# The convolution's first loads move into the attention's last step, and the convolution opens the ternary feedforward

## The chip, the cores and the metric

The kernel runs on one core of a Trainium2 chip. A core has five engines with an instruction stream each: TensorE (PE, matrix products, which write to PSUM), VectorE (DVE), ScalarE (ACT), GpSimd (POOL) and SyncE (SP), which here issues nearly all the DMA transfers. The engines meet only through semaphores. The metric is the device time of one launch in microseconds (us), the median of the runs; lower is better.

## The reference, cut to what matters

The program is a decoder of six stages on x of shape (8, 256, 512), each with a residual and a layer norm. The last three are these; L is 512, because the convolution reads the (8, 256, 512) tensors as (batch, channels, length).

```
def attention1(x):            # 64 heads of 8, softmax over 256 keys, output projection
def convolution(k, v, q):     # k = v = context, q = x; B, HD, L = 8, 256, 512; head_dim 8, H = 32
    kv = einsum('bhil,bhjl->bijhl', k, v)
    y = irfft(rfft(kv, 2 * L) * rfft(ssm_kernel, 2 * L))[..., :L]
    out = einsum('bijhl,bhil->bjhl', y + kv * D, q)
def ternary_feedforward(x):
    h = gelu(silu(bitlinear158(x, w1, b1)))            # 512 -> 2048
    h = layer_norm(h, ln_g, ln_b)
    return bitlinear158(h, w2, b2)                     # 2048 -> 512
def bitlinear158(x, w, b):    # rms_norm of x, rounded to 8 bits by its row's peak; w rounded to -1, 0, 1
    return einsum('bsd,od->bso', act_quant(rms_norm(x)), weight_quant(w)) + b

x = layer_norm(x + attention1(x))
x = layer_norm(x + convolution(context, context, x))
x = layer_norm(x + ternary_feedforward(x))
```

## The kernel before, in words

`program` calls one function for each stage. A stage opens its tensors, runs one block in which each engine has a program written out by hand, and ends in a barrier of all engines; only then does the next stage's first instruction start. The order on each engine is the order of the code.

`attention1` works on eight sequences (B = 8, step b). In its last step SP sends the last two quantised pieces of the ternary weights (`send_piece`, out of `d_wq`), then stores the last four tiles of x (`store_x`) and waits until they have landed (`stored`).

`long_convolution` goes over NT = 16 pairs n of heads, h = 2n and 2n + 1 (SH = 32 heads). For each head, ACT copies contexts (`widen`, into `e_cx`) and puts them into PSUM (`put`, `e_pc`); DVE multiplies them (`products`, into `e_kv`); PE convolves them with a matrix of taps (`convolve`, from `e_toep`, into `e_py`: four PSUM banks, reused one for one, so that unit t of a head waits until DVE has read unit t of the head before); DVE multiplies the result by the queries (`weigh`, `e_qx`, into `e_planes`); ACT completes three small edges (`wraps`); POOL sums the planes (`sums`, in three additions of 1024, 512 and 256 elements a partition). For each pair, PE transposes the rows of x (`turn_x`, into `e_px`) which ACT copies into queries (`queries`), and transposes the sums back (`turn_z`, into `e_pz`) which DVE adds to x (`add`). The layer norm is left to ACT and POOL (`square`, `root`, `normal`). SP loads contexts (`e_ctr`, for two pairs at a time), taps and rows of x (`x_rows`) in the stage itself. The first convolution of PE stands ahead of its first `turn_x`.

`ternary_feedforward` takes 16 tiles of 128 rows in groups of GT = 4, as a software pipeline written as steps s, from -3 on. The opening of a group is: ACT squares the rows of its four tiles (`g_junk_x`), DVE takes their peaks (`group_peaks`), POOL makes a reciprocal root, DVE works out scales (`group_scales`, nine small operations in a row), and PE transposes them into `lrows`. The opening of a tile is: DVE scales and rounds it (`g_xq`), PE transposes it, ACT copies it (`g_q1f`), PE forms the first product (`g_p`: four matmuls with the bias in `g_bpart`, sixteen with `g_w`, into four PSUM banks), ACT applies silu and then gelu (`g_ha`). After that DVE and ACT do the layer norm (`g_hc`, `g_junk`), DVE rounds again, PE transposes and forms the second product (`g_pout`). Ahead of the first product stand the loads of all the weights and rows, the constants, and the split of the bias into a high and a low part (`g_bhigh`, `g_bpart`).

## Time and profile before

| | |
|---|---|
| median of 3 runs | 2001.24 us (1999.72 to 2002.05) |
| the profiled execution | 1995.72 us, span 1993.9 us |
| mean granted TensorE clock | 0.931 of full |
| busy share of the span | PE 87%, DVE 70%, ACT 52%, POOL 29% |
| `attention1` ends, convolution's first instruction | 1540.0, 1542.83 us |
| convolution's last instruction, feedforward's first | 1736.03, 1736.87 us |
| end of the span | 1993.9 us |

Busy shares are means over six stages with different limits, so they name no limit for any one of them. Instants are us from the span's start, and an instant at which one engine waits for another is what counts.

### The profile page before, as it was taken

The numbers are of one execution on the slowest core, as the hardware profiler recorded it, in microseconds if no ns is written. First come the engines' busy times: TensorE is split into PE (matmuls) and PEld (weight loads), VectorE is DVE, ScalarE is ACT, GpSimd is POOL, SyncE is SP. The second block draws the span as 40 slices with busy tenths as digits, with TensorE's granted clock in tenths as the row PEclk, the third lists the DMA queues.
The fourth block names the chain that finished last, engine by engine and source line by source line (L and its number), as shares of the span: only waits on it lengthen the run. The fifth ranks groups of instructions, "written<-read, shape, count | busy, mean of one in ns | idle before, by whom it ended". The sixth has DMA issues, their size and how long they took to land. (4 is left out here: it accounts for less than half of the span.)

```text
span 1993.9 us, 32229 instructions
## 1 busy us (share of the span) xinstructions
PE 1731.0 (87%) x11774; PEld 1339.0 (67%) x11774; DVE 1391.4 (70%) x2867; ACT 1033.5 (52%) x1936; POOL 569.2 (29%) x563
## 2 busy tenths in 40 slices
PE   4489999787869999999999997999996899677886
PEld 2255665423548999999999996788884677434443
DVE  8478888587955566666665655555664788649997
ACT  3426666624415444444444443564663344479995
POOL 6133332144110011001000002242342599723322
PEclk9669999956989999999999998999998899879998
DMA  6498888151612222222222234132232544120001
GB/s 168 41 98 98 94 96 91 35 173 39 216 38 64 57 67 67 78 67 67 77 64 70 77 102 148 68 124 79 75 118 76 134 101 90 54 91 11 22 22 32
DMA packets 148480, 163.87 MB, mean 82 GB/s; under 512 B 46240, under 2 KB 100384, under 8 KB 146528
## 3 DMA queue, kind: packets, MB, share of 16 engines
q1 hardware_dynamic: 143076, 151.85, 33.6%
q10 hardware_dynamic: 5248, 9.96, 1.4%
q8 instruction: 95, 1.56, 0.4%
q14 instruction: 61, 0.50, 0.1%
HBM read 116.86 MB, written 19.48 MB: 68 GB/s over the span
## 5 line engine op out<-in xcount | busy, mean ns | idle before, releaser
L1661 ACT ACTIVATE f_gate<-f_gu 128x256 f32<-128x256 f32 x264 | 98.5, 382 | 268.9 <-PE f_gu L1525 190.4
L1802 DVE TENSOR_TENSOR f_hid<-f_gate,f_gu 128x256 f32<-128x256 f32 x264 | 108.3, 420 | 156.0 <-ACT f_gate L1661 152.1
L570 DVE TENSOR_REDUCE a_rowmax<-a_ring 128x2 f32<-128x512 f32 x256 | 165.1, 687 | 52.5 <-PE a_ring L652 50.2
L2688 PE MATMUL e_py<-e_kv,e_toep 128*128 128x288 f32 x640 | 162.7, 410 | 15.6 <-DVE e_kv L2715 15.3
L523 ACT ACTIVATE a_prob<-a_sT 128x1024 f32<-128x1024 f32 x128 | 130.6, 1027 | 49.2 <-PE a_sT L641 49.2
L2688 PEld LDWEIGHTS e_py<-e_kv,e_toep 128*128 128x128 f32 x640 | 120.6, 192 | 47.7 <-issue 16.2
L1538 PE MATMUL f_gu<-f_lowh,f_bg 128*128 128x256 f32 x704 | 141.3, 283 | 5.2 <-POOL f_lowl L1443 5.0
L1525 PE MATMUL f_gu<-f_xhi,f_wg 128*128 128x256 f32 x704 | 131.4, 284 | 0.0
L1525 PE MATMUL f_gu<-f_xhi,f_wu 128*128 128x256 f32 x704 | 130.6, 283 | 0.0
L1807 DVE TENSOR_TENSOR f_hl<-f_hid,f_hh 128x768 fp32r<-128x768 f32 (+2 forms) x90 | 84.5, 939 | 55.9 <-ACT f_hh L1709 54.8
L1538 PEld LDWEIGHTS f_gu<-f_lowh,f_bg 128*128 128x128 f32 x704 | 115.7, 191 | 9.6 <-POOL f_lowl L1443 5.2
L1562 PE MATMUL f_pout<-f_wd,f_hh 128*128 128x512 f32 x352 | 111.2, 397 | 0.0
L1525 PEld LDWEIGHTS f_gu<-f_xhi,f_wg 128*128 128x128 f32 x704 | 109.8, 191 | 0.0
L1525 PEld LDWEIGHTS f_gu<-f_xhi,f_wu 128*128 128x128 f32 x704 | 109.6, 191 | 0.0
L2070 POOL TENSOR_TENSOR d_prob<-d_prob,d_rinv 128x1024 f32<-128x1024 f32 x32 | 60.4, 1894 | 169.7 <-DVE d_rinv L2364 169.7
L1709 ACT ACTIVATE f_hh<-f_hid 128x768 fp32r<-128x768 f32 (+2 forms) x90 | 74.9, 833 | 62.0 <-DVE f_hid L1802 62.0
L2127 PE MATMUL d_ring<-d_xh,d_w 128*128 128x256 f32 x512 | 97.8, 292 | 9.3 <-DVE d_offset L2401 8.3
L484 POOL TENSOR_TENSOR a_y<-a_y,cb 128x512 f32<-128x512 f32 x48 | 50.0, 1042 | 176.6 <-DVE a_y L552 176.6
L1525 PE MATMUL f_gu<-f_xlo,f_wg 128*128 128x256 f32 x352 | 99.9, 284 | 0.0
L1525 PE MATMUL f_gu<-f_xlo,f_wu 128*128 128x256 f32 x352 | 99.7, 283 | 0.0
L1538 PE MATMUL f_gu<-f_lowl,f_bg 128*128 128x256 f32 x352 | 99.6, 283 | 0.0
L652 PE MATMUL a_ring<-a_ks,a_qs 48*128 48x256 f32 x512 | 63.2, 324 | 40.1 <-DVE a_rowmax L570 20.5
(424 smaller groups left out, 4830.7 us busy)
## 6 DMA issues: line engine op xcount, KB each, us to landing
f_entry<-in_WdT SPq DMA_DIRECT2D x89, 256.0 KB, 2.8
d_staging<-in_w SPq DMA_DIRECT2D x16, 1024.0 KB, 5.7
a_qs<-a_hi SPq DMA_DIRECT2D x64, 128.0 KB, 7.4
a_ks<-a_hi SPq DMA_DIRECT2D x64, 128.0 KB, 6.0
e_toep<-lags SPq DMA_DIRECT2D x16, 512.0 KB, 3.8
f_entry<-in_Bg SPq DMA_DIRECT2D x89, 64.0 KB, 1.8
f_entry<-in_Bu SPq DMA_DIRECT2D x89, 64.0 KB, 2.0
cf<-in_xT SPq DMA_DIRECT2D x4, 1024.0 KB, 7.8
```

Source lines behind the costliest of these rows:

```text
L523: act.activation(prob[:, n % 4, :, :, :], sT[n % 2][:, :, :, :], ACT.Exp).then_inc(exp_done, 1)
L570: dve.tensor_reduce(rowmax[:, s % 2, :, e * SLOTS + j], ring[n % RING][:, :].rearrange("p (q t) -> p q t", t=T), AX.X, ALU.max, negate=Tru ...
L652: last = pe.matmul(dst[e][:, q * T:(q + 1) * T], qs[par][rows, pair, q * P:(q + 1) * P], ks[par][rows, pair, :], start=True, stop=True)
L1525: last = pe.matmul(gu[n % 3][:, w, :], ws[hw][:, k, f * P:(f + 1) * P], xs[b % 2][:, k, :], start=(m == 0 and w == 0), stop=(m == 3 * KT - ...
L1538: last = pe.matmul(gu[n % 3][:, w, :], bg[:, n % BR, h, w, :], xs[:, u, j - 1, w, :], start=False, stop=True, skip_group_check=True)
L1562: last = pe.matmul(pout[q][:, :], xs[:, t % 2, 0, cols], wd[:, n % WR, h, :], start=(f == 0 and m == 0), stop=(f == FT - 1 and m == 2))
L1661: act.activation(gate[:, i % 2, :], gu[n % 3][:, 0, :], ACT.Silu).then_inc(s_["gate_ready"], 1)
L1709: act.activation(hh[:, t % 2, lo:hi, :], hid[:, lo:hi, :], ACT.Copy).then_inc(s_["hh_ready"], 1)
L1802: dve.tensor_tensor(hid[:, j, :], gate[:, i % 2, :], gu[n % 3][:, 1, :], ALU.mult).then_inc(s_["hid_ready"], 1)
L1807: dve.tensor_tensor(hl[:, t % 2, lo:hi, :], hid[:, lo:hi, :], hh[:, t % 2, lo:hi, :], ALU.subtract).then_inc(s_["hl_ready"], 1)
L2127: last = pe.matmul(dst[:, f * T:(f + 1) * T], w[hw][:, wi, k, o * P:(o + 1) * P], xs[:, k, :], start=(m == 0), stop=(m == 3 * KT - 1))
L2688: last = pe.matmul(py[n % RING][:, 0:YS], toep[:, u, h % 2, (t - j) * P:(t - j + 1) * P], kv[:, h % 2, j, :, :].rearrange("p b c -> p (b c ...
```

## The change

Three things are changed. First, in the last step of `attention1` SP issues the convolution's first eight context loads and three loads of taps, once the last `v1` has been read; after the last store of x has landed it issues the first four loads of rows. In the convolution PE does `turn_x(0)` ahead of its first convolution. Second, SP issues the feedforward's loads within the convolution, one a pair from pair 4 on. Third, the convolution does the feedforward's opening: the constants and the split of the bias, squares for tiles 0 to 11, peaks and scales for tiles 0 to 3, the rounding and the transposes of tile 0, and, after its last convolution, the first product of tile 0. The feedforward then starts at step 0 with silu of tile 0. The four banks of `e_py` become those of the product, so the profile of the changed kernel calls them g_p.

The core of the diff:

```diff
+                    if b == B - 1:
+                        sp.wait_ge(s_["ring_read"], ring_at["v1", b] + 1)
+                        sp.wait_ge(s_["orow_added"], B * TB)
+                        sp.wait_ge(stored, 16 * (B - 2) * TB)
+                        for m in range(2):
+                            loads.contexts(sp, io, m)
+                        for n in range(CR):
+                            loads.taps(sp, io, n)
...
+                sp.wait_ge(stored, 16 * B * TB)
+                for n in range(4):
+                    loads.tokens(sp, io, n)
                 for u in range(2):
                     sp.wait_ge(sent_w[u], 16 * KT)
-                sp.wait_ge(stored, 16 * B * TB)
...
+                    if 4 <= n < 4 + 2 * KT + 3:
+                        ternary_load(n - 4)
...
+                    if n == 8:
+                        pool.wait_ge(s_["t_ssq"], GT)
+                        pool.tensor_scalar(g["meansq"][:, first], g["ssq"][:, first], 1.0 / D, EPS, ALU.mult, ALU.add
+                                           ).then_inc(s_["t_meansq"], 1)
...
+                    if 3 <= n < 3 + 3 * GT:
+                        q = n - 3
+                        act.wait_ge(s_["x_ready"], q + 1)
+                        act.activation(g["junk_x"][:, q % GT, :], rows[:, q, :], ACT.Square, accum_out=g["ssq"][:, q:q + 1]
+                                       ).then_inc(s_["t_ssq"], 1)
+                    if n == 1:
+                        act.wait_ge(s_["b1_in"], 16)
+                        act.activation(bhigh[:, :], brow[:, :], ACT.Copy).then_inc(s_["t_bhigh"], 1)
...
+                turn_x(0)
                 for n in range(NT):
                     convolve(2 * n)
-                    if n == 0:
-                        turn_x(0)
...
+                    if n == 10:
+                        pe.wait_ge(s_["t_lift"], 1)
...
+                pe.wait_ge(s_["z_ready"], SH * KT)
+                pe.wait_ge(s_["t_loaded"], 16 * (2 * KT + 3))
+                pe.wait_ge(s_["t_bpart"], 2)
+                ternary_products(pe, g, 0).then_inc(s_["t_h"], 1)
                 turn_z(NT - 1)
...
+                    if 4 <= n < 4 + GT:
+                        dve.wait_ge(s_["x_ready"], n - 3)
+                        dve.tensor_reduce(g["peak"][:, n - 4:n - 3], rows[:, n - 4, :], AX.X, ALU.max, apply_absolute_value=True
+                                          ).then_inc(s_["t_peak"], 1)
+                    if n in (2, 3):
...
+                    if n == 9:
+                        dve.wait_ge(s_["t_root"], 1)
+                        dve.wait_ge(s_["t_peak"], GT)
+                        group_scales(dve, Chain(dve, s_["t_steps"]), g, wmean, first, s_["t_fore"], s_["t_lift"])
+                    if n == 10:
...
-    STEPS = range(-3, NT + LAST)
+    STEPS = range(NT + LAST)
```

SP's queue where the attention passes into the convolution, before (`d_wq` are the weights that are sent, `x<-d_x` the stores of x):

```order
L2030 DMA ternary<-d_wq 128x2048 x2
L2034 DMA x<-d_x 128x512 x4
L2006 UNCONDITIONAL_BRANCH
L2533 UNCONDITIONAL_BRANCH
L2539 DMA e_ctr<-in_ctxRev 128x8x32 x4
L2547 DMA e_toep<-lags 128x2x512
L2552 DMA x_rows<-x 128x1x512
L2547 DMA e_toep<-lags 128x2x512
L2552 DMA x_rows<-x 128x1x512
L2539 DMA e_ctr<-in_ctxRev 128x8x32 x4
```

And now:

```order
L1950 DMA e_ctr<-in_ctxRev 128x8x32 x8
L1956 DMA e_toep<-lags 128x2x512 x3
L2066 DMA ternary<-d_wq 128x2048 x2
L2070 DMA x<-d_x 128x512 x4
L1959 DMA x_rows<-x 128x1x512 x4
L2042 UNCONDITIONAL_BRANCH
L2641 UNCONDITIONAL_BRANCH
L2657 DMA g_brow<-in_b 4x2048
```

The two branches are the end of one block and the beginning of the next. Eleven loads stand ahead of the last two sends, and four behind the last store.

DVE in pair 9 of the changed convolution, between `weigh(18)` and `products(20)`, which followed each other directly before:

```order
L2885 TENSOR_TENSOR e_planes<-g_p,e_qx 128x8x3x8
L2540 TENSOR_TENSOR g_top<-g_peak,g_xroot 128x4
L2541 TENSOR_SCALAR g_top<-g_top 128x4
L2542 TENSOR_SCALAR g_back<-g_top,g_wmean 128x4
L2544 RECIPROCAL g_inv<-g_top 128x4
L2545 SCALAR_TENSOR_TENSOR g_fore<-g_inv,g_xroot 128x4
L2546 TENSOR_SCALAR g_lift<-g_inv,g_wfac 128x4
L2547 CAST g_lhigh<-g_lift 128x4
L2549 COPY g_lcols<-g_lhigh 128x4x2
L2551 TENSOR_TENSOR g_lcols<-g_lift,g_lhigh 128x4x2
L2866 TENSOR_TENSOR e_kv<-e_pc,e_cx 128x32x32
```

The nine rows of `group_scales` used to stand at the feedforward's start.

PE at the end of the convolution and the beginning of the feedforward, before:

```order
L2688 MATMUL e_py<-e_kv,e_toep 128x288 x20
L2674 MATMUL e_pz<-ident,e_zf 128x128 x8
L2532 UNCONDITIONAL_BRANCH
L2953 UNCONDITIONAL_BRANCH
L3017 MATMUL g_pq<-ident,g_lcols 4x128 x4
L2978 MATMUL g_pq<-ident,g_xq 128x128 x8
L3002 MATMUL g_p<-g_bpart,g_lrows 128x512 x4
L3006 MATMUL g_p<-g_w,g_q1f 128x512 x16
L2978 MATMUL g_pq<-ident,g_xq 128x128 x4
L3002 MATMUL g_p<-g_bpart,g_lrows 128x512 x4
L3006 MATMUL g_p<-g_w,g_q1f 128x512 x16
```

And now:

```order
L2826 MATMUL g_p<-e_kv,e_toep 128x288 x20
L2812 MATMUL e_pz<-ident,e_zf 128x128 x4
L2559 MATMUL g_p<-g_bpart,g_lrows 128x512 x4
L2563 MATMUL g_p<-g_w,g_q1f 128x512 x16
L2812 MATMUL e_pz<-ident,e_zf 128x128 x4
L2640 UNCONDITIONAL_BRANCH
L3100 UNCONDITIONAL_BRANCH
L3125 MATMUL g_pq<-ident,g_xq 128x128 x8
L2559 MATMUL g_p<-g_bpart,g_lrows 128x512 x4
L2563 MATMUL g_p<-g_w,g_q1f 128x512 x16
```

The first product stands between the last two transposes of `e_zf`; behind the barrier the transposes of tiles 1 and 2 come first, then the product of tile 1.

## Rows read from the trace of the kernel before

**Rows 1.** Timeline, 1500 to 1530: start us, us, engine, line, operation [idle before <-releaser]

```profile
1502.14 0.69 DVE L2369 TENSOR_TENSOR d_v<-d_ring,d_vrow 128x512 f32<-128x512 f32 x1 [2.14 <-PE d_ring L2137]
1515.93 10.01 SPq L2030 DMA_DIRECT2D ternary<-d_wq  x2
```

**Rows 2.** Timeline, 1539 to 1567: the attention's end and the convolution's first pair

```profile
1542.83 2.85 SPq L2539 DMA_DIRECT2D e_ctr<-in_ctxRev  x4
1547.62 0.61 SPq L2552 DMA_DIRECT2D x_rows<-x  x1
1548.27 7.64 SPq L2539 DMA_DIRECT2D e_ctr<-in_ctxRev  x4
1548.64 0.63 ACT L2613 ACTIVATE e_cx<-e_ctr 128x512 f32<-128x512 f32 x1 [20.17 <-DMA e_ctr<-in_ctxRev]
1551.59 7.24 PE L2688 MATMUL e_py<-e_kv,e_toep 128*128 128x288 f32 x20 [15.34 <-DVE e_kv L2715]
1566.48 0.36 SPq L2547 DMA_DIRECT2D e_toep<-lags  x1
```

**Rows 3.** Windows, 1661 to 1672: busy us (x) PE, PEld, DVE, ACT, POOL, clock, DMA, GB/s

```profile
1661.00:1672.00 11.00, 11.00 (x53) 8.75 (x52) 9.64 (x32) 4.93 (x15) 10.04 (x10) 1.00 0.23 73
```

**Rows 4.** Timeline of one pair, 1613 to 1620

```profile
1618.73 0.60 PE L2674 MATMUL e_pz<-ident,e_zf 128*128 128x128 f32 x4
1619.17 5.02 PE L2688 MATMUL e_py<-e_kv,e_toep 128*128 128x288 f32 x20
...
1614.38 1.22 DVE L2713 TENSOR_TENSOR e_kv<-e_pc,e_cx 128x1024 f32<-128x1024 f32 x1
1616.44 0.42 DVE L2729 TENSOR_TENSOR e_planes<-e_py,e_qx 128x256 f32<-128x256 f32 x1
1618.94 0.42 DVE L2729 TENSOR_TENSOR e_planes<-e_py,e_qx 128x256 f32<-128x256 f32 x1 [0.96 <-PE e_py L2688]
...
1615.50 2.36 POOL L2568 TENSOR_TENSOR e_planes<-e_planes 128x1024 f32<-128x1024 f32 x1 [0.41 <-ACT e_planes L2627]
```

**Rows 5.** Timeline, 1260 to 1263: DVE beside POOL

```profile
1260.74 1.90 POOL L2070 TENSOR_TENSOR d_prob<-d_prob,d_rinv 128x1024 f32<-128x1024 f32 x1 [14.78 <-DVE d_rinv L2364]
1261.87 0.79 DVE L2359 TENSOR_SCALAR d_shift<-d_nmax 128x4 f32<-128x4 f32 x1
```

**Rows 6.** Instructions by tile: ns min/median/max, first and last start

```profile
L2359 DVE TENSOR_SCALAR d_shift<-d_nmax x32: 170/172/791, 1254.7 to 1511.3; 128x4 f32<-128x4 f32 x32
L952 DVE TENSOR_TENSOR x_rows<-a_r,x_rows x5: 692/1781/1785, 440.9 to 468.3; 128x512 f32<-128x512 f32 x5
```

**Rows 7.** Timeline, 1731 to 1737: the convolution's end

```profile
1731.12 1.11 PE L2674 MATMUL e_pz<-ident,e_zf 128*128 128x128 f32 x4 [6.45 <-POOL e_zf L2572]
1735.22 0.81 ACT L2636 ACTIVATE x_rows<-x_rows,e_stats 128x512 f32<-128x512 f32 x1 [1.21 <-POOL e_stats L2583]
1736.87 0.30 SPq L2845 DMA_DIRECT2D g_brow<-in_b  x1
```

**Rows 8.** Timeline, 1750 to 1782: the feedforward's opening

```profile
1750.40 2.07 PE L3002 MATMUL g_p<-g_bpart,g_lrows 4*128 4x512 f32 x4
1758.49 1.97 ACT L2902 ACTIVATE g_ha<-g_p,g_back 128x2048 f32<-128x2048 f32 x1 [4.93 <-PE g_p L3006]
1761.05 1.28 ACT L2906 ACT_TABLE_LOAD   x1
1765.66 1.97 ACT L2902 ACTIVATE g_ha<-g_p,g_back 128x2048 f32<-128x2048 f32 x1
1773.41 1.94 ACT L2902 ACTIVATE g_ha<-g_p,g_back 128x2048 f32<-128x2048 f32 x1
1781.13 0.62 ACT L2913 ACTIVATE g_junk_x<-x_rows 128x512 bf16<-128x512 f32 x1
```

**Rows 9.** Windows in the feedforward: busy us (x) PE, PEld, DVE, ACT, POOL

```profile
1758.00:1845.00 87.00, 64.45 (x298) 33.01 (x296) 61.29 (x75) 77.83 (x88) 30.17 (x36) 0.91 0.03 7
1845.00:1970.00 125.00, 103.85 (x519) 55.17 (x518) 122.76 (x147) 114.66 (x129) 37.93 (x71) 0.94 0.09 22
```

More of the change, by code:

```diff
@@ L1923, with __init__, semaphores, contexts @@
 STAGES.append(expert_feedforward)
+CR = 3
+class ConvolutionLoads:
+    def __init__(self, nc, start, rows_at):
+        mk = Maker(nc, None)
+        self.size = 2 * KT * B * 4 * SD * 4 + CR * 2 * D * 4
+        self.start = start
+        self.ctr = mk.at(start, "e_ctr", [P, 2, KT, B, 4 * SD])
+        self.toep = mk.at(start + 2 * KT * B * 4 * SD * 4, "e_toep", [P, CR, 2, D])
+        self.rows_at = rows_at
+        self.rows = mk.at(rows_at, "x_rows", [P, N // P, D])
+        self.got_c = [nc.alloc_semaphore(name=f"e_got_c{u}") for u in range(2)]
+        self.got_t = [nc.alloc_semaphore(name=f"e_got_t{u}") for u in range(CR)]
+        self.got_x = [nc.alloc_semaphore(name=f"e_got_x{u}") for u in range(4)]
+    def semaphores(self):
+        return self.got_c + self.got_t + self.got_x
+    def contexts(self, sp, io, m):
+        for k in range(KT):
+            sp.dma_start(self.ctr[:, m % 2, k, :, :], io["ctxRev"][k * P:(k + 1) * P, :].rearrange(
+                "p (b m s) -> m p b s", b=B, s=4 * SD)[m]).then_inc(self.got_c[m % 2], 16)
+    def taps(self, sp, io, n):
+        row = io["lags"][2 * n:2 * n + 1, :]
+        window = bass.AP(tensor=row.tensor, offset=row.offset + 1, ap=[[1, P], [P + D, 2], [1, D]])
+        sp.dma_start(self.toep[:, n % CR, :, :], window).then_inc(self.got_t[n % CR], 16)
+    def tokens(self, sp, io, n):
+        sp.dma_start(self.rows[:, n, :], by_heads(io["x4"], n)).then_inc(self.got_x[n % 4], 16)
 def attention1(nc, io, sem, keep):
@@ new lines, in ternary_products @@
+def ternary_products(pe, g, t):
+    for n in range(INNER // 512):
+        pe.matmul(g["p1"][:, n * 512:(n + 1) * 512], g["lrows"][:, t // GT % 2, t % GT * P:(t % GT + 1) * P],
+                  g["bpart"][:, n * 512:(n + 1) * 512], start=True, stop=False)
+    for n in range(INNER // 512):
+        for j in range(KT):
+            last = pe.matmul(g["p1"][:, n * 512:(n + 1) * 512], g["q1f"][:, t % 2, j, :], g["w1"][:, j, n * 512:(n + 1) * 512],
+                             start=False, stop=(j == KT - 1))
+    return last
@@ L2479, in long_convolution @@
     RING = 4
-    CR, QR, ZR = 3, 3, 2
-    own_rows = Maker(nc, keep["ternary"]["held"]).sb("x_rows", [P, NT, D])
-    keep["ternary"]["rows"] = rows = own_rows
+    QR, ZR = 3, 2
+    loads = keep.pop("loads")
+    ctr, toep, rows = loads.ctr, loads.toep, loads.rows
+    Maker(nc, keep["ternary"]["held"]).sb("x_rows_place", [P, NT, D])
+    keep["ternary"]["rows"] = rows
+    keep["ternary"]["early"] = g = ternary_early(nc, keep["ternary"]["held"])
+    wmean, winv = keep["ternary"]["wmean"], keep["ternary"]["winv"]
+    first = slice(0, GT)
     with ExitStack() as ctx:
         mk = Maker(nc, ctx)
-        ctr = mk.sb("e_ctr", [P, 2, KT, B, 4 * SD])
+        place = mk.sb("e_loads", [P, loads.size // 4])
+        assert nc.lookup_mloc(place).addr == loads.start, (nc.lookup_mloc(place).addr, loads.start)
         cx = mk.sb("e_cx", [P, CR, KT, B, 2, WIDE])
@@ L2549, in tokens @@
-                def tokens(n):
+                        loads.taps(sp, io, n)
                     if n >= 4:
                         sp.wait_ge(s_["x_turned"], n - 3)
-                    sp.dma_start(rows[:, n, :], by_heads(io["x4"], n)).then_inc(got_x[n % 4], 16)
-                contexts(0)
-                for n in range(NT):
-                    taps(n)
-                    tokens(n)
-                    if n % 2 == 1 and n + 1 < NT:
-                        contexts(n // 2 + 1)
+                        loads.tokens(sp, io, n)
```

270 lines of the change are left out of this document (140 added, 130 removed).

## The prediction

> **What bounds the kernel now.** I read the page first, then the timelines around the two stage boundaries, then a table of windows through the last three stages. The page only says that PE is busy for most of the span. The two boundaries say where the change can act.
>
> At the first boundary SP issues the convolution's first load at 1542.83, ACT can copy contexts at 1548.64, PE starts at 1551.59 after 15.34 us of idleness, and the first pair is over when SP is released for the next taps at 1566.48 [rows 2]. At the second, the last activation of the convolution ends at 1735.22 + 0.81 = 1736.03 and the feedforward's first instruction comes at 1736.87, so the barrier takes 0.84 us [rows 7]. The first product begins at 1750.40 and the first silu only at 1758.49 [rows 8]: 21.6 us after the feedforward's first instruction, in which no tile is worked on beyond its opening.
>
> Between the boundaries PE is busy for 11.00 of 11 us, but DVE for 9.64 and POOL for 10.04 too [rows 3]. A convolution's price is PE's; work added to DVE or POOL is free only within their small slack. Behind the second boundary the feedforward is first ACT's (77.83 of 87 us), then DVE's (122.76 of 125) [rows 9]. Neither changes its steady work, so what comes earlier at the start comes out earlier at the end.
>
> **The start of the convolution: 5.7 us less.** Before, the last store has landed one barrier ahead of 1542.83, at 1541.99. Now four loads of rows are issued first, 0.61 us each [rows 2] with a little between them, 2.5 us, then the barrier: ACT copies from 1545.4 on instead of 1548.64, since the contexts are there. That is 3.2 us. The first pair took from 1551.59 to 1566.48, 14.9 us. Its first convolution takes 7.1 of them (7.24 less the overlap of the last matmul); the second should take the 4.85 of a convolution at full clock (5.02 in its row, less that overlap), and the transposes between them 0.44, the distance from 1618.73 to 1619.17 [rows 4]. 12.4 in place of 14.9 is 2.5 less: `turn_x(0)` ahead of the first convolution gives DVE its queries while PE convolves, and the second convolution no longer waits for DVE. DVE's first `products` hide that early transpose if the rows land within some 3.5 us.
>
> Can SP issue the eleven early loads without holding something? The last `v1` is read at 1502.8, and the next send waits until 1515.93 [rows 1]. Four contexts in a full queue took 7.64 us, four in an empty one 2.85 [rows 2]; eight and the taps thus take between 7 and 16 us, 13 by what the same loads need now. They may end at 1516, at worst at 1519. The send behind them is late by that; the one after it waits for a quantisation until about 1525.6 anyhow (1515.93 + 10.01, less its issue). Cost: nothing.
>
> **PE's added work in the convolution: 0.9 us more.** Four transposes each in pairs 10 and 11, at 0.44. The product of tile 0 lies after the last convolution, where PE sat idle for 6.45 us until 1731.12 [rows 7]. It needs 4.8 us at full clock: in the stage now, silu to silu is 7.75 us (1765.66 to 1773.41) with a silu of about 2 and the rest the product and a transpose [rows 8]. So it ends about 1 us before `turn_z(15)` can start. Without that cover it would cost its 4.8. Because PE is no longer idle there, the last transposes should take about 0.6 instead of 1.11: 0.5 less.
>
> **DVE's added work in the convolution: 5.2 us more.** This is the term about which I am least sure. First the slack. An insertion stands in front of the 1614.38 row of [rows 4]. DVE finishes unit 0 of the next head at 1616.44, and PE's following convolution, at 1619.17, needs it: 2.7 us to spare. DVE itself waits 0.96 us for PE once a head later on, so a delay under about 1 us is gone in the same pair. Four peaks (0.57 each, a quarter of the four tiles' reduction), the two halves of the split (1.2 each) and the rounding (0.5) stay under 2.7. They cost at most the odd 0.2; I book 0.4 in all.
>
> `group_scales` is nine small operations, 1.6 us if nothing holds them, and then free too. But a DVE operation of just this kind (tensor and scalar, 128x4, 0.17 us) takes 0.79 when it starts within POOL's tensor_tensor: 1261.87 + 0.79 = 1262.66, and POOL's ends at 1262.64 [rows 5]. Its range is 170 to 791 ns [rows 6]. An addition of two SBUF tensors takes 1781 ns instead of 692 beside POOL [rows 6]. So such an operation waits until POOL's current one is over; then POOL's next starts almost at once and the next small one waits again. Eight of the nine are of these kinds (I leave out the reciprocal). In the convolution POOL has operations of 2.36, 1.27 and 0.73 us in a row, from 1615.50 [rows 4]. From 1614.38 on: two or three of the eight pass before 1615.5, the others get through behind 2.36, 1.27, 0.73 and the three short ones of `root`, so the chain ends some 7.4 us after it began. Less the slack of 2.7 that is 4.7, and the DVE then lags, 0.1 more: 4.8. The bounds are 0 (none held) and 6 (all behind full operations). I take 4.8, because the nearest row in shape shows the hold in every digit.
>
> The Trainium skill, GPSIMD Engine Reference, in the table at its head, says that GpSimd shares its SBUF interfaces with VectorE, with contention for VectorE instructions in a 2-port mode or with two SBUF inputs. By that rule the trace agrees, and the sum is as given; without it the sum would be 4.8 us lower.
>
> ACT's added squares (0.62 each in the feedforward now [rows 8]) and copies fit: ACT is busy for 4.93 of 11 us [rows 3]. POOL's root for four tiles (about 1.3 us) stands between two sums; it delays a head by less than DVE's 0.96, and the last pairs make it up, 0.41 a pair [rows 4].
>
> **The feedforward: 18.0 us less.** From its first instruction (call it 0): a table load of 1.28 as in [rows 8], so silu(0) at 1.4. It ends at 3.35; the copy of tile 1 takes 0.65; then PE transposes tile 2, which stands ahead of the product of tile 1, at low clock 1.2 with its hand-over (1.11 in [rows 7]); then the product to the next silu at a low granted clock, 8.09 as between 1750.40 and 1758.49 [rows 8]. silu(1) is at 13.3, silu(2) 7.75 later at 21.05. Before, silu(2) came at 1773.41 - 1736.87 = 36.54. That is 15.5 less. It isn't the 20 us by which silu(0) moves, since the product of tile 1, formerly warm, is now the cold one. Then the four squares from 1781.13 on, 2.5 us on an ACT that waits for nothing there, have been done in the convolution: 2.5 less. From there both orders are the same.
>
> **The sum.** -5.7 + 0.9 - 0.5 + 5.2 - 18.0 = -18.1 us. Against the profiled execution, 1995.72, that is 1977.6. The median of the runs shown, 2001.24, is 5.5 above that execution; on it, 1983.1.
>
> **The rivals.**
>
> The scales are not held (25%). For: the hold is seen with a whole POOL operation of 1.9 us and one small one, never with a chain of them; and some of the nine may be of another kind. Then 4.8 less: 1978.3.
>
> The early loads arrive late, or the stage doesn't turn into a steady pair at once (12%). The rows of pair 0 are read back 2 us after they were stored; if they land 4 us later than I assume, PE's first `turn_x` holds the first convolution and the start gives 1.7 in place of 5.7: 1987.1.
>
> The feedforward gives back a part (12%). DVE is busy 122.76 of 125 us later; if it, not ACT, already limits from silu(4) on, the 2.5 of the squares are lost, and with PE's clock falling once more in the first tiles (a product costs 3.3 us more then: 8.09 for 4.8) the gain is 5.8 less: 1988.9.
>
> Slower than before (3%): the feedforward's loads, 6.5 MB (eight of 512 KB, two of 1 MB, one of 256 KB), share the queue with the convolution's taps. A taps load is issued two pairs, 21 us, ahead of its use, and PE, busy for 11.00 of 11 us [rows 3], never waits for one now. Only if a load took over 21 us would PE wait, and it would have to wait over 1.5 us in each of twelve pairs to eat 18 us; then 2003 or more. Against it: the DMA engines are busy a quarter of the time in such a pair [rows 3].
>
> My forecast holds the remaining 48%. The others all lie within 1978 to 1989, and a few us belong to the state of the chip, so 8 in 10 lie between 1975 and 1991. A measurement of this kernel tells 0.2%, 4 us, from no change. The cases of over 4 us make 0.95 together (I take something off for a mechanism that I don't see), within it 0.02, slower 0.03.
>
> **What would show it right or wrong.** In the changed profile: ACT's first copy of contexts about 3 us after the last store has landed, with no wait for DMA; the first pair at 12 to 13 us; pairs at 10.6 us (twice 4.85 and 0.44), but for one at 15 (pair 9), in which PE waits for `e_kv` and DVE's small rows read 0.8 to 2.4 us instead of 0.2; the product of tile 0 ended before the last sums; silu(0) at 1.4 us, silu(1) at 13 and silu(2) at 21 us behind the feedforward's first instruction. If pair 9 is as long as the others, the held chain is wrong. If PE waits for a DMA in the convolution, the loads are.

## The result

The changed kernel takes 1984.35 us (median of 4 runs, 1983.47 to 1984.86), the kernel before 2000.48 (4 runs beside them, 1995.65 to 2002.05). The ratio is 0.9915 with a 95% interval from 0.9888 to 0.9941: 16.1 us by the medians, where 18.1 were forecast. The time itself had been forecast as 1983.1. That it is hit within 1.3 us, while the gain is off by 2.0, is luck: the kernel before came out 0.8 lower than the 2001.24 that the forecast started from.

The profiled execution has 1984.86 us, span 1983.1. Its span is only 10.8 us below that of the kernel before, since the stages ahead of the change took 3.88 us longer in it: the last `v1` row of DVE begins at 1506.02, before at 1502.14 [rows 1]. That belongs to the execution and not to the change (the fourteen profiles of this study put the attention's last DVE row anywhere between 1537.6 and 1544.2). From the `v1` row on, 14.7 us are won. The tables below therefore compare stages, not spans.

**The start of the convolution.** Timeline of the changed kernel, 1505 to 1567, with rows as in [rows 2]:

```profile
1506.73 6.98 SPq L1950 DMA_DIRECT2D e_ctr<-in_ctxRev  x8
1546.13 2.52 SPq L1959 DMA_DIRECT2D x_rows<-x  x4
1550.12 0.63 ACT L2732 ACTIVATE e_cx<-e_ctr 128x512 f32<-128x512 f32 x1 [17.36 <-PEq L3291]
1550.24 1.12 PE L2804 MATMUL e_px<-ident,x_rows 128*128 128x128 f32 x4 [9.55 <-DMA x_rows<-x]
1553.14 7.17 PE L2826 MATMUL g_p<-e_kv,e_toep 128*128 128x288 f32 x20 [1.78 <-DVE e_kv L2868]
1565.62 0.38 SPq L1956 DMA_DIRECT2D e_toep<-lags  x1
```

ACT no longer waits for a DMA but for the barrier (PE's sequencer). The eight contexts were issued in 6.98 us in the attention. From the first convolution to SP's release it is 12.48 us (14.89 in [rows 2], 12.4 forecast).

**The long pair.** Timeline of the changed kernel, 1655 to 1665. DVE's small operations stand above POOL's:

```profile
1656.03 1.16 DVE L2541 TENSOR_SCALAR g_top<-g_top 128x4 f32<-128x4 f32 x1
1657.22 0.77 DVE L2542 TENSOR_SCALAR g_back<-g_top,g_wmean 128x4 f32<-128x4 f32 x1
1657.91 0.16 DVE L2544 RECIPROCAL g_inv<-g_top 128x4 f32<-128x4 f32 x1
1658.10 2.18 DVE L2545 SCALAR_TENSOR_TENSOR g_fore<-g_inv,g_xroot 128x4 f32<-128x4 f32 x1
1660.46 1.18 DVE L2547 CAST g_lhigh<-g_lift 128x4 fp32r<-128x4 f32 x1
1662.70 1.22 DVE L2866 TENSOR_TENSOR e_kv<-e_pc,e_cx 128x1024 f32<-128x1024 f32 x1 [0.24 <-DVE g_lcols L2551]
...
1655.89 1.27 POOL L2681 TENSOR_TENSOR e_planes<-e_planes 128x512 f32<-128x512 f32 x1
1657.24 0.73 POOL L2684 TENSOR_TENSOR e_zf<-e_planes 128x256 f32<-128x256 f32 x1
1657.93 2.35 POOL L2680 TENSOR_TENSOR e_planes<-e_planes 128x1024 f32<-128x1024 f32 x1
1660.35 1.27 POOL L2681 TENSOR_TENSOR e_planes<-e_planes 128x512 f32<-128x512 f32 x1
...
1664.99 7.56 PE L2826 MATMUL g_p<-e_kv,e_toep 128*128 128x288 f32 x20 [4.20 <-DVE e_planes L2885]
```

Read the ends. L2541 ends at 1657.19 and POOL's L2681 at 1657.16; L2542 at 1657.99 and L2684 at 1657.97; L2545 at 1660.28 and L2680 at 1660.28; L2547 at 1661.64 and L2681 at 1661.62. So does a fifth, L2551, whose 0.70 us end at 1662.45, 0.02 behind POOL's L2684. The two engines alternate: a small operation waits out POOL's running one, POOL's next starts, and the next small one waits for that. No semaphore stands between them, so the engines do not meet only through semaphores, as was said of the chip at the outset. The other four (L2540, L2544, L2546 and L2549) took 0.15 to 0.22 us; all four began 0.02 to 0.14 us ahead of POOL's next operation. From 1655.85, the chain's first row, to `e_kv` it is 6.85 us (7.4 forecast), of which the five held rows make 5.98. The Trainium skill, SBUF — State Buffer, section "SBUF: two separate sides", calls the port pair that DVE and GpSimd share an exclusive lock that is held for a whole instruction; by that rule, the trace agrees to 0.03 us five times.

Windows of the same stretch (busy us and count of PE, PEld, DVE, ACT, POOL, then the granted clock):

```profile
1660.00:1664.80 4.80, 0.80 (x6) 0.46 (x4) 4.49 (x11) 0.00 (x0) 3.21 (x6) 0.83 0.63 151
1664.80:1667.00 2.20, 2.01 (x4) 1.50 (x5) 2.20 (x11) 0.00 (x0) 0.00 (x0) 0.50 0.89 194
1667.00:1669.00 2.00, 2.00 (x6) 1.38 (x5) 1.97 (x6) 1.72 (x6) 1.29 (x1) 0.50 0.24 88
1669.00:1671.00 2.00, 2.00 (x8) 1.51 (x7) 2.00 (x9) 1.97 (x6) 1.92 (x2) 0.75 0.00 0
```

After 4.20 us of idle PE the granted clock is 0.50, the lower level (1.2 GHz), and the row of one convolution is 7.56 us long instead of 5.02 [rows 4]. The pair lasts 17.48 us (SP's `e_toep` rows at 1660.39 and 1677.87) instead of 10.58: 6.90 more.

**The second boundary.** Timeline, 1732 to 1765, as in [rows 7] and [rows 8]:

```profile
1732.08 1.18 PE L2559 MATMUL g_p<-g_bpart,g_lrows 4*128 4x512 f32 x4 [0.47 <-DVE e_planes L2885]
1738.08 0.65 PE L2812 MATMUL e_pz<-ident,e_zf 128*128 128x128 f32 x4 [1.26 <-POOL e_zf L2684]
1741.97 0.81 ACT L2755 ACTIVATE x_rows<-x_rows,e_stats 128x512 f32<-128x512 f32 x1 [1.22 <-POOL e_stats L2695]
1743.91 1.28 ACT L3047 ACT_TABLE_LOAD   x1 [1.12 <-PEq L3291]
1750.91 5.79 PE L2563 MATMUL g_p<-g_w,g_q1f 128*128 128x512 bf16 x16
1756.74 1.97 ACT L3047 ACTIVATE g_ha<-g_p,g_back 128x2048 f32<-128x2048 f32 x1 [3.80 <-PE g_p L2563]
1764.48 1.94 ACT L3047 ACTIVATE g_ha<-g_p,g_back 128x2048 f32<-128x2048 f32 x1
```

The product of tile 0 is over 1.26 us before PE may go on, and the last transposes take 0.65 us in place of 1.11. silu(1) is at 12.83 and silu(2) at 20.57 us behind the first instruction, 1743.91 (36.54 before; 13.3 and 21.05 forecast).

### The profile page after: what moved, and what is told of

It is laid out like the page before. It is cut to its first block and busy times, and to the rows that moved or that the text cites. A ratio compares the mean times of both kernels' runs of the same rounds, so it can differ in the third digit from the quotient of the medians.

```text
span 1983.1 us, 32214 instructions
## 1 busy us (share of the span) xinstructions
PE 1737.2 (88%) x11756; PEld 1345.4 (68%) x11774; DVE 1398.1 (71%) x2871; ACT 1034.5 (52%) x1936; POOL 571.6 (29%) x563
## 5 line engine op out<-in xcount | busy, mean ns | idle before, releaser
L2826 PE MATMUL g_p<-e_kv,e_toep 128*128 128x288 f32 x640 | 164.9, 415 | 6.0 <-DVE e_planes L2885 4.2
L2826 PEld LDWEIGHTS g_p<-e_kv,e_toep 128*128 128x128 f32 x640 | 122.2, 195 | 38.7 <-issue 6.6
```

Source lines behind the costliest of these rows:

```text
L2826: last = pe.matmul(py[n % RING][:, 0:YS], toep[:, u, h % 2, (t - j) * P:(t - j + 1) * P], kv[:, h % 2, j, :, :].rearrange("p b c -> p (b c ...
```

## The experiments

"Boundary 1" runs from the start of the attention's last DVE row to the end of pair 0, "convolution" from there to the end of its last activation, "opening" from there to silu(2), "rest" from silu(2) to the end of the span. Sum is that of the four; all are us of one profiled execution. Medians and ratios are against runs of the kernel before beside them, whose median was 1996.97 to 2000.48; the medians of different rows are within each other's range where they differ by 2 or 3 us.

| kernel | boundary 1 | convolution | opening | rest | sum | median | ratio, 95% interval |
|---|---|---|---|---|---|---|---|
| before | 27.38 | 169.55 | 37.38 | 220.49 | 454.80 | | |
| changed | 22.08 | 177.16 | 21.70 | 218.62 | 439.56 | 1984.35 | 0.9915 [0.9888, 0.9941] |
| e11 changed, again | 21.94 | 177.05 | 21.68 | 218.56 | 439.23 | 1982.86 | 0.9924 [0.9905, 0.9944] |
| e1 POOL yields | 21.96 | 171.28 | 21.14 | 218.02 | 432.40 | 1974.33 | 0.9883 [0.9865, 0.9900] |
| e2 PE kept busy | 21.90 | 174.84 | 21.08 | 217.91 | 435.73 | 1977.46 | 0.9896 [0.9880, 0.9912] |
| e3 four pieces | 22.04 | 170.24 | 21.70 | 218.81 | 432.79 | 1975.88 | 0.9893 [0.9872, 0.9914] |
| e4 turn late | 24.21 | 177.62 | 21.91 | 218.76 | 442.50 | 1986.39 | 0.9936 [0.9919, 0.9954] |
| e5 loads late | 28.04 | 177.42 | 21.84 | 218.75 | 446.05 | 1985.34 | 0.9921 [0.9893, 0.9950] |
| e6 squares back | 21.91 | 177.06 | 27.83 | 222.58 | 449.38 | 1994.03 | 0.9964 [0.9943, 0.9986] |
| e7 PE warm into feedforward | 21.91 | 177.07 | 18.94 | 217.84 | 435.76 | 1977.49 | 0.9887 [0.9854, 0.9920] |
| e8 e3 and e7 | 21.91 | 170.26 | 18.95 | 218.00 | 429.12 | 1975.05 | 0.9877 [0.9847, 0.9907] |
| e9 product back | 22.06 | 177.47 | 28.51 | 218.40 | 446.44 | 1991.67 | 0.9966 [0.9952, 0.9980] |
| e10 e8, tiles 2, 3 warm | 21.88 | 170.23 | 18.94 | 217.95 | 429.00 | 1973.19 | 0.9878 [0.9858, 0.9899] |
| e12 e8, tile 4 warm | 21.88 | 170.23 | 18.93 | 218.99 | 430.03 | 1975.24 | 0.9882 [0.9858, 0.9906] |

**e11: what repeats.**

> The changed kernel without any edit, a second time. It asks which differences between two profiles belong to the execution. Theory (the stages before the change vary by some 4 us from execution to execution, for both kernels; the convolution and the feedforward are the same within 0.5 us each time): the last v1 row of DVE comes between 1500 and 1507, from there to the end of pair 0 it takes 59 to 60 us, the pairs are 10.58 each with one of 17.4 to 17.9 and two of 11.0, and silu(2) comes at 20.4 to 20.9 us. Rival (the long pair's length depends on how POOL and DVE happen to meet): it lies outside 17.0 to 18.0 us.

The four stages repeat within 0.15 us, the long pair is 17.40. The pairs are not all 10.58: SP is late with one issue of taps, so two neighbouring ones read 11.77 and 9.39, together twice 10.58. The part ahead of boundary 1 differs by 0.6 us from the first profile and by up to 6.6 between others. Even so two profiles alike don't give the scatter of a column. In e1 and e2 the opening is 0.6 us shorter and the rest 0.6 to 0.7, though their edits act in the convolution alone: the second part of tile 1's product is 5.25 us long in e1 and 5.79 in the changed kernel, because the granted clock rises earlier in it, and silu(3) to silu(4) is 8.49 and 8.45 in place of 9.20. So in the last two columns 0.7 us can belong to the moment at which the clock rises, and a difference of 3 us between two medians means little.

**e1: is the chain held by POOL?**

```diff
                 for n in range(NT):
+                    if n == 9:
+                        pool.wait_ge(s_["t_lift"], 1)
                     sums(2 * n)
```

> The changed kernel with one edit: POOL waits for the end of group_scales (t_lift) before its first sum of pair 9, so that no POOL operation runs beside the nine small DVE operations. Theory (they are held by POOL, each until POOL's running operation is over): the chain takes about 2 us in place of the 6.85 of the changed kernel's profile (its nine rows there are 0.15 to 2.18 us each), every small row is below 0.3 us, and the long pair (17.48 us) falls to about 11 to 12, since 2 us lie within DVE's slack of 2.7 us; POOL is late by about 2 us, which may cost 0 to 2 us in the next pair. The whole is 5 to 7 us below the changed kernel's profiled 1984.9, if the stages before take the same time. Rival (the operations are slow by themselves, or wait for their own semaphores): the chain stays at 6 to 7 us, the pair stays at 17 us or grows by what POOL is late, and nothing is won.

Timeline of e1, 1652 to 1658:

```profile
1652.46 1.15 DVE L2541 TENSOR_SCALAR g_top<-g_top 128x4 f32<-128x4 f32 x1
1654.53 0.16 DVE L2545 SCALAR_TENSOR_TENSOR g_fore<-g_inv,g_xroot 128x4 f32<-128x4 f32 x1
1654.87 0.17 DVE L2547 CAST g_lhigh<-g_lift 128x4 fp32r<-128x4 f32 x1
...
1652.32 1.27 POOL L2681 TENSOR_TENSOR e_planes<-e_planes 128x512 f32<-128x512 f32 x1
1653.67 0.73 POOL L2684 TENSOR_TENSOR e_zf<-e_planes 128x256 f32<-128x256 f32 x1
1655.45 2.35 POOL L2680 TENSOR_TENSOR e_planes<-e_planes 128x1024 f32<-128x1024 f32 x1 [1.06 <-DVEq L2553]
```

Two operations are still held by the sums that POOL had begun before its wait (1.15 and 0.77 us); once POOL is silent, the same L2545 takes 0.16 in place of 2.18 and L2547 0.17 in place of 1.18. The chain is 3.28 us long, not 2 as expected, the pair 11.63, and the convolution 5.9 us shorter; 1.2 us more of the sum are in the opening and the rest, which e1 doesn't touch. The hold is shown, and the rival (slow by themselves) is out.

**e2: is a part of it the clock?**

```diff
+                    if n == 9:
+                        pe.wait_ge(s_["q_ready"], 2 * (n + 2))
+                        for q in range(36):
+                            pe.transpose(px[:, 0:P], keep["ident"][:, :], keep["ident"][:, :])
                     if n == 10:
                         pe.wait_ge(s_["t_lift"], 1)
```

> The changed kernel with one edit: at the end of pair 9 PE transposes the identity 36 times into the bank of the row transposes, which nobody reads (the first transposes of pair 10 overwrite it), while it would otherwise wait for DVE. The chain of small operations is not touched. Theory (of the 6.9 us of the long pair 4.2 are PE's wait and 2.7 are the matmuls' lower clock behind it, granted 0.50 and 0.75 instead of 1.00): with PE kept busy the granted clock stays at 1.00, the next convolution takes 4.9 us rather than 7.56, and the long pair takes 14.5 to 15 us rather than 17.48, that is 2.5 to 2.7 us less. Rival (the convolution behind the wait is slow because its inputs arrive late, not for the clock): it stays at 7.6 us and the pair at 17.5.

Timeline of e2's PE, 1655 to 1666:

```profile
1655.98 4.09 PE L2841 MATMUL e_px<-ident 128*128 128x128 f32 x36
1660.34 5.27 PE L2826 MATMUL g_p<-e_kv,e_toep 128*128 128x288 f32 x20 [0.27 <-DVE e_planes L2889]
```

The granted clock stays at 1.00, the convolution behind the wait takes 5.27 in place of 7.56, the pair 15.19 in place of 17.48. (5.27 is also the length of that row in e1, where the clock stays at 1.00 as well, so it belongs to a start behind a wait.) So 2.3 of the 6.9 us are the clock and go away with useless work; the other 4.6 are PE's wait itself. Of the 3.8 us in the sum the remaining 1.5 are, but for 0.2, again the opening and the rest.

**e3: does a chain in pieces fit the slack?** `group_scales` is cut into four functions of two or three operations, and they are moved from ahead of `products` to behind `add`, the last of DVE's work in a pair:

```diff
+                    if n == 9:
+                        dve.wait_ge(s_["t_root"], 1)
+                        dve.wait_ge(s_["t_peak"], GT)
+                    if 9 <= n < 13:
+                        pieces[n - 9]()
                 add(NT - 1)
```

> The changed kernel with group_scales cut into four pieces of two or three operations, one at the end of each of pairs 9 to 12, and the rounding, the two sets of transposes and the two copies of ACT three pairs later. Theory (the hold costs what exceeds DVE's slack of 2.7 us once): each piece is held for 1 to 3.6 us at most, so nearly all lies within the slack, no pair is longer than 12 us, and the 6.9 us of the long pair are won, less up to 1 for pieces that are held by a whole sum: 6 to 7 us below the changed kernel. Rival (what is added to DVE costs its own time wherever it stands, since DVE is nearly always busy): the four pairs together are 5 to 7 us longer than normal ones, and at most 1 to 2 us are won, by the clock alone.

All pairs from 9 on are 10.57 to 10.58 us, so from pair 0 to pair 12 it is 126.50 us, exactly what the kernel before needs. Windows of e3, pairs 9 and 10, columns as above:

```profile
1656.50:1667.10 10.60, 10.60 (x50) 8.40 (x49) 10.06 (x34) 5.63 (x17) 10.04 (x10) 1.00 0.49 130
1667.10:1677.70 10.60, 10.60 (x51) 8.40 (x50) 9.77 (x35) 5.66 (x17) 10.04 (x10) 1.00 0.78 173
```

PE is busy throughout. But the pieces were also hardly held. Windows of this length in the kernel before have 9.47 us of DVE, so 0.6 and 0.3 us were added, not the 1 to 3.6 that the expectation allowed a piece. Timeline of e3's DVE:

```profile
1658.06 0.54 DVE L2561 TENSOR_TENSOR g_top<-g_peak,g_xroot 128x4 f32<-128x4 f32 x1
1679.46 0.17 DVE L2572 CAST g_lhigh<-g_lift 128x4 fp32r<-128x4 f32 x1
```

Only the first of the nine is held, up to the end of a sum of POOL at 1658.59. The others take 0.16 to 0.22 us each. Behind `add` POOL is at the short operations of `root`, and the cast, held for 1.18 us by a sum in the changed kernel, here passes inside one of them (L2720, 128x1, 1679.25 to 1679.84). So e3 shows that the same nine operations cost nothing where they now stand. Whether pieces that are held would fit into the slack, or whether the whole chain in the new place would do as well, it doesn't show: cutting and moving were not tested apart. The transposes now lie in pairs 13 and 14 (0.44 each); with them the whole convolution is 0.7 us longer than in the kernel before.

**e4 and e5: what the start is made of.**

```diff
-                turn_x(0)
                 for n in range(NT):
                     convolve(2 * n)
+                    if n == 0:
+                        turn_x(0)
```

> The changed kernel with turn_x(0) back behind the first convolution, as in the kernel before; all else is kept. Theory (2.4 of the 5 us won at the start of the convolution come from this order: DVE has its queries while PE convolves): PE's first matmul comes no later, or up to 1 us earlier since it no longer waits for the rows (the transposes began only when x_rows landed), but the first pair takes 14.9 us rather than 12.48. The whole is 1.5 to 2.4 us slower than the changed kernel. Rival (the first pair is shorter only because its loads are there): the pair stays at 12.5 us and the time is the same or 1 us less.

e5 removes the loads from the attention and writes them at the head of the convolution's SP program:

```diff
+                loads.contexts(sp, io, 0)
+                for n in range(CR):
+                    loads.taps(sp, io, n)
+                    loads.tokens(sp, io, n)
+                    if n == 1:
+                        loads.contexts(sp, io, 1)
+                loads.tokens(sp, io, 3)
                 sp.dma_start(brow[:, :], io["b1"].broadcast_to([4, INNER])).then_inc(s_["b1_in"], 16)
```

> The changed kernel with all early loads (contexts, taps and tokens) back in the convolution's own block, in the order of the kernel before, with the early turn_x(0) and the opened feedforward kept. Theory (what the early loads bring is ACT's start, since the contexts are there after the barrier, less the 2.5 us of the rows' issue ahead of it): from the last DVE row of the attention to PE's first convolution 11 to 12 us, in place of 9.05 and near the 11.94 of the kernel before; the first pair stays at 12.4 to 12.5 us. Together 2.5 to 3.2 us slower than the changed kernel between that row and the end of pair 0. Rival 1 (the early loads cost the attention's last step as much as they bring: it was 0.56 us longer): the step is 0.5 us shorter and the net is 2 us or less. Rival 2 (the rows, now landing after the contexts, hold turn_x(0) and so the first convolution): 4 us or more.

In e4 PE's first convolution comes as early as in the changed kernel (9.58 us behind DVE's last row, 9.60 there) and the first pair takes 14.63 us, so the theory holds: 2.1 us slower. Boundary 1, in us:

| | turn after the first convolution | turn ahead of it |
|---|---|---|
| loads in the convolution | 27.38 (before) | 28.04 (e5) |
| loads in the attention | 24.21 (e4) | 22.08 (changed) |

The early loads win in both columns, 3.2 us alone and 6.0 with the early turn. The early turn wins 2.1 us only where the loads are early, and loses 0.7 where they aren't. With late loads the rows land last, and PE stands before them although `e_kv` has been ready since 1549.96. Timeline of e5:

```profile
1549.68 0.28 DVE L2865 TENSOR_TENSOR e_kv<-e_pc,e_cx 128x128 f32<-128x128 f32 x1
1551.80 1.11 PE L2801 MATMUL e_px<-ident,x_rows 128*128 128x128 f32 x4 [17.11 <-DMA x_rows<-x]
1552.71 3.57 PE L2823 MATMUL g_p<-e_kv,e_toep 128*128 128x288 f32 x7
```

That is the second rival of e5 (6.0 us against 2.5 to 3.2 expected). The attention's last step is not longer for the early loads: 36.8 to 37.5 us in eleven profiles that have them, 37.0 in the kernel before and in e5 (one, e1's, is at 34.9).

**e6: what the squares were worth.**

```diff
-                    if 3 <= n < 3 + 3 * GT:
+                    if 3 <= n < 3 + GT:
...
-                        if g == NG - 1:
-                            pool.wait_ge(s_["ssq1"], GT)
+                        pool.wait_ge(s_["ssq1"], g * GT)
...
-                    if g is not None and g == NG - 1:
+                    if g is not None:
```

> The changed kernel with the squares of tiles 4 to 11 back in the feedforward (four from silu(2) on, four more four tiles later), those of tiles 0 to 3 kept in the convolution. Theory (ACT waits for nothing in the feedforward's first tiles, so four squares of 0.62 us there cost 2.5 us, and the later four too unless DVE limits by then): from silu(2) to the end of the span 2 to 2.5 us more than 218.6, with the second group of four costing nothing; the convolution unchanged. Rival 1 (ACT limits at both places): 4 to 5 us more. Rival 2 (DVE limits from the start, the time behind silu(2) differs between the two kernels for another reason): less than 0.5 us more.

All three theories missed: the feedforward is 10.1 us longer. One reason is that the edit puts the squares of tiles 4 to 7 behind gelu(0) and not behind silu(2), as the expectation has it; those of tiles 8 to 11 are behind silu(2). Between silu(2) and silu(3) it is 13.48 in place of 11.02, the 2.5 us that the prediction had priced; 0.8 more come before silu(4) and 0.7 later. The other 6.1 lie ahead of silu(2). Timeline of e6, 1750 to 1767:

```profile
1750.51 0.20 POOL L3015 TENSOR_SCALAR g_meansq<-g_ssq 128x4 f32<-128x4 f32 x1 [11.66 <-ACT g_junk_x L3066]
1751.84 1.21 DVE L2540 TENSOR_TENSOR g_top<-g_peak,g_xroot 128x4 f32<-128x4 f32 x1 [7.90 <-POOL g_xroot L3016]
1756.55 0.88 DVE L3197 TENSOR_SCALAR g_xq<-x_rows,g_fore 128x512 f32<-128x512 f32 x2
...
1757.09 1.11 PE L3124 MATMUL g_pq<-ident,g_xq 128*128 128x128 f32 x4 [3.51 <-DVE g_xq L3197]
1760.54 6.02 PE L2563 MATMUL g_p<-g_w,g_q1f 128*128 128x512 bf16 x15 [0.33 <-issue]
```

DVE stands in `group_scales(1)` for the root of squares that ACT makes only behind gelu(0); the rounding of tile 3 is queued behind it, PE waits for that, and the product of tile 2 then runs at the low clock. In the kernel before ACT made the squares of tiles 4 to 7 at 1749.14 to 1751.69 and then waited 4.93 us for the first product [rows 8], so there they cost nothing; here they are on the path.

**e7: is the second product cold, and does the end follow?**

```diff
                 turn_z(NT - 1)
+                for q in range(44):
+                    pe.transpose(px[:, 0:P], keep["ident"][:, :], keep["ident"][:, :])
...
+                    if t == 2:
+                        for q in range(20):
+                            pe.transpose(pout[:, 0:P], keep["ident"][:, :], keep["ident"][:, :])
```

> The changed kernel with transposes of the identity that nobody reads: 44 behind the convolution's last transposes, while the engines finish the last rows and the barrier, and 20 in the feedforward ahead of the transposes of tile 2. Theory (the second product costs 7.9 us, 2.07 + 5.79, only because PE had been idle before it): with the granted clock kept at 1.00 the product takes 4.8 us, silu(1) comes at about 9.5 us behind the feedforward's first instruction in place of 12.83, silu(2) at 17 in place of 20.57, and the end follows: 3 to 3.5 us below the changed kernel. Rival (the gain is taken back because the first tiles then wait for DVE or ACT elsewhere): silu(2) earlier by 3 us, but the time from silu(2) to the end longer by 1 to 3.

The product of tile 1 takes 1.19 + 3.40 us in place of 2.07 + 5.79, at a granted clock of 1.00 throughout; silu(2) is at 18.94 behind the convolution's end, 2.76 earlier, although the barrier is 0.73 longer (the 44 transposes end at 1742.38, the last activation at 1741.62). The rest is not longer (217.84), so the end follows. The sum is 3.8 us lower, but of that only the 2.8 us of the opening are shown to be the transposes' work: 0.8 are the rest, as short in e1 and e2, which have none of them. Timeline of e7:

```profile
1748.03 1.19 PE L2559 MATMUL g_p<-g_bpart,g_lrows 4*128 4x512 f32 x4
1749.38 3.40 PE L2563 MATMUL g_p<-g_w,g_q1f 128*128 128x512 bf16 x15 [0.16 <-issue]
```

The Trainium skill, TensorE: Matmul & The Clock Gate, section "What's actually happening", has it that the low clock is the default and activity releases it. By that rule the traces of e2 and e7 agree: work that nobody reads does it as well as work that is needed.

**e8: do both gains add?** The edits of e3 and e7 together.

> The kernel with the scales in four pieces over pairs 9 to 12 (no pair longer than the others there) and the transposes of the kernel that keeps PE busy into the feedforward, both together. If both mechanisms are right and act at places that do not touch each other, their gains add: 6.9 from the first and 3 to 3.5 from the second, that is 10 us below the changed kernel and 24 to 26 below the kernel before, ratio 0.987 to 0.988. If PE's filling at the convolution's end holds the last transposes, or the clock falls somewhere else for the additional work, 6 to 7 us below the changed kernel.

By stages they add: 10.4 us below the changed kernel (6.8 and 3.8 alone), 25.7 below the kernel before. By medians the ratio is 0.9877 against 0.9915 and 0.9924 of the changed kernel, and not to be told from e3's or e7's own.

**e9: what the product of tile 0 brings.** `ternary_products(0)` moves from the convolution's end to the head of the feedforward's PE program, and the counts of `h_done` go up by one.

> The changed kernel with only the product of tile 0 back at the start of the feedforward; its scales, its rounding, its transposes, its copies and all loads stay in the convolution. It asks which part of the 15.97 us won at the opening comes from this product. Theory (whichever product is first in the feedforward runs at the low clock, since PE was idle before it, and the next one is then warm): silu(0) comes at 8 to 9 us behind the feedforward's first instruction in place of 1.29, silu(1) at 15 to 17 in place of 12.83 and silu(2) at 23 to 24.5 in place of 20.57. So the product alone brings 2.5 to 4 us, and the other 12 come from what precedes it (scales, rounding, split). Rival (the product brings its full time of 8 us at the low clock): silu(2) at 28 to 29. At the convolution's end nothing is won: the last transposes take 1.11 us at the low clock again.

Timeline of e9's PE, with the last part of the product of tile 0 and then the product of tile 1:

```profile
1746.83 6.00 PE L2563 MATMUL g_p<-g_w,g_q1f 128*128 128x512 bf16 x15 [0.33 <-issue]
1756.58 2.07 PE L2559 MATMUL g_p<-g_bpart,g_lrows 4*128 4x512 f32 x4
1758.58 5.46 PE L2563 MATMUL g_p<-g_w,g_q1f 128*128 128x512 bf16 x16
```

Silu(2) is 6.8 us later, against 2.5 to 4 expected. Both products run at the low clock for the most part: the granted clock is 1.00 only from the end of the first (1752.8 to 1755.5, in which PE is busy for 0.47 of 2.70 us, waiting for silu(0) and the copy behind it), and it is 0.50 again under the transposes and the product of tile 1. So the rival's price of 8 us was nearer, and 6.8 of the opening's 16 us are this one product.

**e10 and e12: more of the same.** In e10 14 and 36 transposes stand ahead of the products of tiles 2 and 3, in e12 34 ahead of tile 4 alone, otherwise both are e8. "Second part" is the product's sixteen matmuls with `g_w`.

> The kernel that has both gains (scales in four pieces, PE kept busy into the feedforward), with more transposes of the identity that nobody reads: 14 ahead of the product of tile 2 and 36 ahead of that of tile 3, where PE was idle for 1.1 and 4.2 us. Theory (these products are slower for the clock alone: 5.09 and 5.14 us in place of 3.40 and 3.63 for their second part): both take 3.4 to 3.6, ACT's wait ahead of silu(4) falls from 2.0 to about 0.5 us, silu(3) to silu(4) from 8.42 to about 7, so 1.5 us at most, if the end follows. Rival (behind silu(4) DVE limits and takes it back): the silus are earlier by that, but the time from silu(4) to the end grows by as much, and nothing is won.

The products become fast (3.63 and 3.40 us), but no silu moves: ACT wasn't waiting for them, and the one that it waited for, tile 4's, kept its 5.13. I had put the transposes one product too early.

> The kernel that has both gains, with 34 transposes of the identity ahead of the product of tile 4 alone, where PE was idle for 4.17 us and ACT then waited 2.01 us for the product (2.01 ahead of silu(4)); ahead of tiles 2 and 3 nothing is added, since ACT didn't wait there. Theory: the product's second part takes 3.4 to 3.6 us in place of 5.14, ACT's wait ahead of silu(4) falls to 0.3 to 0.6 us, silu(3) to silu(4) is 6.9 to 7.1 us in place of 8.42. Of these 1.5 us the end keeps all if ACT limits on (silu(4) to the end then equal to 189.6 minus nothing), none if DVE does: then the time from silu(2) to the end stays at 218.0.

(The 189.6 in it is a slip; in e8 silu(4) to the end is 198.6.) Timeline of e12's PE:

```profile
1759.32 3.88 PE L3177 MATMUL g_pout<-ident 128*128 128x128 f32 x34
1765.01 3.40 PE L2591 MATMUL g_p<-g_w,g_q1f 128*128 128x512 bf16 x15 [0.16 <-issue]
```

Silu(3) to silu(4) is 6.82 us in place of 8.42, as expected. But the rest is 218.99 against 218.00: all 1.6 us are given back, and 1.0 more. Silu(4) to silu(5) is 17.62 us in place of 15.53: ACT waits 1.25 us for DVE's `g_hc`, and PE 4.95 us for ACT's copies. That row of DVE begins 10.96 us behind silu(3), in e8 10.94, so it didn't move with the silus, and DVE sets the pace there. Silu(7) to silu(8) is another 1.7 us longer and the stretch behind the last silu 1.1 shorter; the cause of these two is open.

## Why the prediction was right, and where its sizes were off

**The start: 5.7 forecast, 4.7 measured.** ACT's earlier start gave 2.9 (3.2 forecast: DVE's last row to PE's first convolution, 12.49 to 9.60) and the shorter pair 2.4 (2.5). From the last DVE row of the attention on these are the 5.3 us of the table's first column. Against them stand 0.6 us of the attention's last step, which was that much longer in this profile than in the one before, within what the others scatter; without it the term is missed by 0.4, not 1.0. The loads cost nothing, as said. That the two halves depend on each other was seen only as a rival (the rows hold `turn_x(0)`); e5 shows what it would have cost.

**PE's added work: 0.9 forecast, 0.87 measured** (pairs 11 and 12 at 11.01 and 11.02). The product was hidden. The last transposes were 0.46 shorter (0.5 forecast), but only 0.2 reached the stage's end: from their start to the end of the last activation it is 4.70 us in place of 4.91. ACT is busy with the layer norm of the pair before until 1740.05 and can't take the last rows earlier. The prediction took it for granted that the end follows.

**DVE's added work: 5.2 forecast, 6.9 measured. This is the mis-sized term.** The mechanism is as written (e1), and the chain's 6.85 us near the 7.4. That it came so near is partly luck: the chain met POOL's 1.27, 0.73, 2.35, 1.27 and 0.73 us, not 2.36, 1.27, 0.73 and the short ones of `root`, one of which didn't hold the cast in e3. PE's wait, 4.2 us in its row and 4.6 in the pair of e2, was booked as the whole price. The clock falls during it and takes 2.3 more (e2). The prediction counted the low clock at both stage boundaries and forgot it inside the pair where it forecast 4.7 us of idleness itself. The 0.4 for peaks, split and rounding was not needed: no other pair is longer.

**The barrier** ahead of the feedforward took 1.13 in place of 0.84; no step had it. In e7 it is 1.86, but only 1.10 from the end of PE's transposes, which are there the last to end.

**The feedforward: 18.0 forecast, 17.8 measured**, with 16.0 (15.5) up to silu(2) and 1.9 (2.5) behind it. The squares gave 2.45 up to silu(3) and 0.4 up to silu(4), of which 1.0 is given back, all of it behind the last silu (56.79 us from there to the end, 55.78 before); why is open. Its size was right, its reasons incomplete: the prediction booked 2.5 us for the squares, and with two groups of them back 10.1 of the gain are lost (e6). It also had the product of tile 1 as cold, and e7 confirms that.

In sum: -4.7 + 7.6 + 0.3 - 16.0 - 1.9 = -14.7 in the profiles, where 7.6 is the convolution from pair 0 on; -18.1 was forecast. Of the difference of 3.4 some 2.0 are the convolution (7.6 for 5.6: 1.7 DVE's term, 0.3 the last transposes), 1.0 the start, 0.3 the barrier and 0.2 the feedforward.

None of the rivals came true as a whole. e3 is what the first described (scales that cost nothing), made by moving them. What stays open: why the medians (16.1) show more than the stages of the two profiles (14.7); with 3.9 us between two executions of the same stages, that can't be settled from single profiles.

## What to carry to other kernels

A chain of small DVE operations beside POOL's large additions costs the sum of POOL's operations, not its own 1.6 us. Spread over four rounds, at a place where POOL has only short operations, it was free (6.9 us to 0); which of the two did it, the spreading or the place, is not shown, so look at what POOL does beside the new place. Wherever a wait of some us is forecast for PE, add what the matmuls behind it lose at the low clock, and ask whether useless transposes could keep it up; but only ahead of a product that somebody waits for. When a change moves a preparation forward, test its parts in pairs: here the early turn without the early loads loses 0.7 us, and the opened feedforward without the moved squares of tiles 4 to 11 loses 10 of its 18.

## What the runs showed that I had not expected

Only some of DVE's operations are held. The large products of `e_kv`, which read `e_pc` in PSUM, kept their 1.22 us beside POOL: in the changed kernel one begins at 1667.78, inside POOL's sum of 1667.71 to 1670.07. Whether the reciprocal is of that kind isn't shown. It took 0.16 us, but it began 0.02 us ahead of POOL's sum (1657.91 and 1657.93), and so did the copy L2549 (1661.67 and 1661.69), which took 0.17. Which of the two engines begins first thus seems to matter, and no run sets it apart.

The convolution behind the wait ran from 1664.99 to about 1672.5, of which 4.2 us had a granted clock of 0.50 and the next 2.0 one of 0.75. Half of 4.2 and a quarter of 2.0 are 2.6, an estimate of what the clock cost; e2 measured 2.3.
